# Moving the keys' products and sums of a seven-level complex scan from VectorE to GpSimd

## What is computed

```python
c = jax.lax.complex(qkva[..., 0], qkva[..., 1])
q, k, v, a = (c[..., 0], c[..., 1], c[..., 2], c[..., 3])
mag2 = a.real * a.real + a.imag * a.imag
a = a * (jax.lax.rsqrt(mag2) * jax.nn.sigmoid(jnp.log(mag2)))
kv = jnp.einsum('blhd,blhe->blhde', k, v)
...
def comb(c1, c2):
    a1, x1 = c1
    a2, x2 = c2
    return (a1 * a2, a2 * x1 + x2)
_, h = jax.lax.associative_scan(comb, (a_e, kv), axis=1)
y = jnp.einsum('blhd,blhde->blhe', q, h)
```

## Time and profile before

| | |
|---|---|
| time, median of 3 runs | 3893.76 us (3890.83 to 3897.11) |
| profiled execution, its own time | 3925.24 us |
| span of the profiled execution | 3923.4 us |
| TensorE busy | 2883.7 us (73%) |
| VectorE busy | 2113.1 us (54%), 4928 instructions |
| ScalarE busy | 928.3 us (24%) |
| GpSimd busy | 652.6 us (17%), 682 instructions |
| mean granted TensorE clock | 0.78 of full speed |
| L2075 (scores), per head group | 205.6 and 203.4 us busy, 232.2 and 226.2 us idle before |

### The profile page before, as it was taken

One profiled execution on the slowest core, in us unless ns is written; L12 is line 12 of the kernel. 1 busy time (PEld: TensorE's weight loads), 2 busy tenths in 40 slices (PEclk: granted clock), 3 DMA queues, 4 the chain that ended last, 5 costly groups with the idle time before them and its releaser, 6 DMA issues.

```text
span 3923.4 us, 112483 instructions
## 1 busy us (share of the span) xinstructions
PE 2883.7 (73%) x51136; PEld 2151.2 (55%) x51136; DVE 2113.1 (54%) x4928; ACT 928.3 (24%) x1820; POOL 652.6 (17%) x682
## 2 busy tenths in 40 slices
PE   4268669867885898488749875986678466999990
PEld 3254357435743674466447545743564346888880
DVE  4446766576658556856685577658543841000004
ACT  0212133113311431142223213311321131222220
POOL 0314200410060006002500330042000000000006
PEclk8578767867786878587858776886769578999995
DMA  2122201210021122012201220121011005555545
GB/s 78 22 55 49 45 3 50 65 30 33 30 66 20 40 39 59 10 39 50 49 9 40 60 45 4 44 65 32 9 46 41 4 15 189 198 195 191 197 156 174
DMA packets 230141, 249.52 MB, mean 64 GB/s; under 512 B 147360, under 2 KB 187168, under 8 KB 227360
## 3 DMA queue, kind: packets, MB, share of 16 engines
q1 hardware_dynamic: 223520, 225.54, 20.1%
q0 software_dynamic: 6144, 16.79, 1.4%
HBM read 196.15 MB, written 46.14 MB: 62 GB/s over the span
## 4 chain that ended last, share of the span: by engine, by line
PE 63%; issue 14%; DVE 8%; POOL 5%; ACT 4%; DMA 1%; SPq 0%; POOLq 0%; DVEq 0%
PE bank L1780 13%; PE bank L2075 10%; PE bank L2278 7%; PE bank L2297 7%; PE bank L2013 4%; POOL arena L1672 3%; PE bank L2090 2%; PE bank L2095 2%; PE bank L1790 2%; PE bank L1907 2%; POOL arena L1716 2%; PE bank L1912 2%; PE bank L1917 1%; PE bank L2035 1%; PE bank L1886 1%
## 5 line engine op out<-in xcount | busy, mean ns | idle before, releaser
L1672 POOL TENSOR_TENSOR arena<-arena 128x1 f32<-128x1 f32 (+30 forms) x496 | 435.1, 907 | 639.4 <-DMA arena<-n_d 467.9
L2075 PE MATMUL bank<-arena 32*32 32x32 f32 (+1 forms) x13824 | 205.6, 253 | 232.2 <-issue 226.0
L2075 PE MATMUL bank<-arena,xn 32*32 32x32 f32 (+1 forms) x13824 | 203.4, 258 | 226.2 <-issue 226.2
L1693 POOL DMA_INDIRECT h_d<-h_tok,pos_now x64 | 66.2, 1035 | 1753.5 <-DVE pos_now L1537 1736.5
L1128 DVE TENSOR_REDUCE arena<-arena 128x1 f32<-128x1 f32 (+30 forms) x496 | 243.7, 502 | 173.3 <-POOL arena L1672 168.9
L1780 PE MATMUL bank<-hT,ring 128*128 128x512 f32 x640 | 316.1, 647 | 8.2 <-DVE arena L1272 8.2
L2075 PEld LDWEIGHTS bank<-arena 32*32 32x32 f32 x13824 | 181.8, 134 | 254.3 <-issue 241.2
L2075 PEld LDWEIGHTS bank<-arena,xn 32*32 32x32 f32 x13824 | 179.3, 135 | 242.6 <-issue 242.1
L2278 PE MATMUL bank<-arena 128*128 128x256 f32 x1248 | 276.6, 380 | 0.0
L2297 PE MATMUL bank<-arena 128*128 128x256 f32 x1248 | 275.6, 379 | 0.0
L2278 PEld LDWEIGHTS bank<-arena 128*128 128x128 f32 x1248 | 237.7, 191 | 32.8 <-issue 0.4
(11 more groups left out here) (332 smaller groups left out, 5185.8 us busy)
## 6 DMA issues: line engine op xcount, KB each, us to landing
arena<-in_w_ring SPq DMA_DIRECT2D x78, 1024.0 KB, 5.0
ring<-in_w_ring SPq DMA_DIRECT2D x104, 512.0 KB, 4.9
arena<-h_d SPq DMA_DIRECT2D x39, 256.0 KB, 5.3
y_d<-arena SPq DMA_DIRECT2D x39, 256.0 KB, 5.8
n_d<-NA SPq DMA_DIRECT2D x8, 1024.0 KB, 3.9
arena<-n_d SPq DMA_DIRECT2D x16, 512.0 KB, 8.1
u_d<-arena SPq DMA_DIRECT2D x8, 1024.0 KB, 3.8
NA<-u_d SPq DMA_DIRECT2D x32, 256.0 KB, 5.9
```

What stands on the lines that cost most here:

```text
L1672: pool.tensor_tensor(part, Usub[:, c, 0:t, 0:t], Nsub[:, c, t, 0:t].unsqueeze(1).to_broadcast([P, t, t]), ALU.mult)\
L2075: i_ = mm(bank[4 * hg + h][keys, b * width:(b + 1) * width], K2[rows_, r, b, keys], q, start=(r == 0), stop=(r == 1), skip_group_check=True)
```

## The change

The two key products and the two key sums of each step are issued on GpSimd instead of VectorE, in a loop behind the clearing of the score buffers. They write the same buffers u1 and u2. GpSimd waits for the table (`a_ok`), for the key planes in level 0, for its own previous results, and for `scored` before the sums; it now raises `k_ready`. SyncE and ScalarE, which waited for `k_ready` alone, wait for VectorE's `q_ready` too, since both engines have to be through. Queries, tables, masked copies and all matmuls are as before.

```diff
@@ sync
                 if pre and rest:
                     sp.wait_ge(*at(k_ready, 1))
+                    sp.wait_ge(*at(q_ready, 2 * HG + 1))
                     load_next()
@@ scalar
                     act.wait_ge(*at(k_ready, HG * LEVELS))
+                    act.wait_ge(*at(q_ready, HG * (STEPS + 1)))
@@ vector
-                        Ta = w[:, :, :, 1]
-                        kk = K2s[hg][:, :, :, :].rearrange(half, two=2, m=m)[:, :, :, 0]
-                        if lev == 0:
-                            dve.wait_ge(*at(plane_ok, 6 * hg + 6))
-                        dve.tensor_tensor(tmp(u1), kk, over(Ta[:, 0]), ALU.mult).then_inc(*up(dve_step, me))
-                        dve.tensor_tensor(tmp(u2), kk, over(Ta[:, 1]), ALU.mult).then_inc(*up(dve_step, me))
                         settle()
                         dve.wait_ge(*at(scored, 2 * (lev + 1) + hg + 1))
                         step(dve.tensor_tensor(q_hi, tmp(t1), tmp(t2), ALU.add))
                         dve.tensor_scalar(q_lo[:, 0], q_hi[:, 1], -1.0, None, ALU.mult).then_inc(*up(q_ready, me))
-                        dve.tensor_tensor(kk[:, 0], tmp(u1)[:, 0], tmp(u2)[:, 1], ALU.subtract)
-                        dve.tensor_tensor(kk[:, 1], tmp(u1)[:, 1], tmp(u2)[:, 0], ALU.add).then_inc(*up(k_ready, me))
@@ gpsimd
+                    def turn_key_columns(hg, lev):
+
+                        m = 1 << lev
+                        w = level_table(hg, lev).rearrange("p r (j two) -> p r j two", two=2)
+                        later = w[:, :, :, 1]
+                        kk = K2s[hg][:, :, :, :].rearrange("p r b (n two m) -> p r (b n) two m", two=2, m=m)[:, :, :, 0]
+
+                        def over(v):
+                            return v.unsqueeze(1).unsqueeze(3).to_broadcast([P, 2, NT // (2 * m), m])
+
+                        v1, v2 = [u[:, :, 0:NT // 2].rearrange("p r (n m) -> p r n m", m=m) for u in (u1, u2)]
+                        if lev == 0:
+                            pool.wait_ge(*at(plane_ok, 6 * hg + 6))
+                            pool.wait_ge(*at(a_ok, hg + 1))
+                        else:
+                            pool.wait_ge(*at(a_ok, 2 * lev + hg + 1))
+                        settle()
+                        pool.tensor_tensor(v1, kk, over(later[:, 0]), ALU.mult).then_inc(*up(key_part, me))
+                        pool.tensor_tensor(v2, kk, over(later[:, 1]), ALU.mult).then_inc(*up(key_part, me))
+                        settle()
+                        pool.wait_ge(*at(scored, 2 * (lev + 1) + hg + 1))
+                        pool.tensor_tensor(kk[:, 0], v1[:, 0], v2[:, 1], ALU.subtract)
+                        pool.tensor_tensor(kk[:, 1], v1[:, 1], v2[:, 0], ALU.add).then_inc(*up(k_ready, me))
+
+                    for lev, hg in itertools.product(range(LEVELS), range(HG)):
+                        turn_key_columns(hg, lev)
```

More of the change, by code:

```diff
@@ L329, in build @@
         u_in = signal("u_in", nxt=64)
-        dve_step = signal("dve_step", rest=226, nxt=13, pre=36)
+        dve_step = signal("dve_step", rest=198, nxt=13, pre=36)
         pre_var = signal("pre_var", pre=1)
@@ L434, in build @@
         k_ready = signal("k_ready", rest=14)
+        key_part = signal("key_part", rest=28)
         numbered = signal("numbered")
@@ L1552, in turn @@
                              q_ready, masked, state_ok, hsq_ok, rt_var, rt_gap, hot_ok,
-                             pos_ok, k_ready])
+                             pos_ok])
                 dve.sem_inc(started.handle, 1)
@@ L1700, in turn @@
                     settle()
-                counted(seg, [zeroed, sub_mul])
+                counted(seg, [zeroed, sub_mul, key_part, k_ready])
                 pool.sem_inc(started.handle, 1)
```

## The result

The changed kernel takes **3939.57 us** (median of 4 runs, 3922.45 to 3942.26) against 3892.30 for the kernel before on the same chip (3890.12 to 3897.11). The ratio is 1.0108, with an interval of [1.0081, 1.0134]: slower by some 42 to 47 us, where 55 were forecast. Run again on another chip, the ratio was 1.0105 [1.0089, 1.0122].

What follows compares the result with a forecast made beforehand. TensorE's own issue paces levels 0 to 4, and the scan's tail decides the change. 48 us of tail plus 7 of clock make 55, against the median 3893.76 giving 3949 us (+1.4%); range 3902 to 4000.

Steps and rivals of the forecast that it cites:

- The bound of the scan's body: Levels 0 to 4: TensorE's own issue sets the pace, 7.5 us a step; lag stays under 4.8 us of margin.
- Freed time on VectorE: 28 us per segment leave VectorE, but only two key sums before the last copies count: 0.67 us, 5.4 in eight.
- GpSimd's own cost: Key work on GpSimd: 1.27 us per 512-element product, 0.73 per 256-element sum, 4.0 us a step.
- Exclusion and alternation: VectorE's two-SBUF-input instructions and GpSimd's reads take turns, so a late step needs 2.59 plus 4.0, together 6.6 us.
- The rival without exclusion: Both engines run side by side in the scan, leaving only the 0.67 us gain: 3888.4 us; chance 0.09.
- the one in which VectorE wins each contest: Rival: in the scan's tail GpSimd is held off and step 11's key sum is late: 11 us, 3905; chance 0.17.
- The tail, 6.0 us a segment: Scan's end: taking turns puts VectorE's step 12 query signal 22.7 us after step 9's query sum; 48 us in all.
- Who ends it: Last copies to first outputs take 20 us instead of 14.3, ended by VectorE's query signal and not by ScalarE.
- The clock, 0.9 us a segment: After a longer pause the outputs' first microseconds may run at TensorE's low clock: 0 to 1.7 us, 7 in all.
- The covers: SyncE's load, ScalarE's waits and GpSimd's row scatter move at no cost; uncovered, each would cost 1 to 3 us per segment.
- The sum: Whole kernel: 48 us plus 7 make 55 us, giving 3949 us (+1.4%).
- The dear GpSimd: Rival: GpSimd at 1.2 times the rows or winning each contest, levels 0 to 2 overflow: 3975 to 4000; chance 0.19.

Runs made afterwards that it cites:

- early: Changed kernel with the key work of levels 5 and 6 back on VectorE, levels 0 to 4 on GpSimd; ratio to the kernel before 0.9986.
- late: Changed kernel with only the key work of levels 5 and 6 on GpSimd, the first ten steps back on VectorE; ratio to the kernel before 1.0097.
- nokeys: Changed kernel with all key products and key sums left out, GpSimd only raising the signals; ratio to the kernel before 0.9987.
- copies_first: Kernel before, all work on VectorE, with each step's masked copies ahead of its two key sums; ratio to the kernel before 0.9986.
- hold: Kernel before, with TensorE waiting before the output products for VectorE's last query signal (step 13) instead of step 12's; ratio 1.0101.
- again: The unchanged kernel before, run once more as if it were a change, for a second profiled execution; ratio 1.0002.

## Why the prediction was right, point by point

**The bound of the scan's body**: right. 699.8 against 699.9 us, within some 5 us, and early and late show the margin holding.

**Freed time on VectorE**: right. 0.67 us a segment, 5.4 in all; nokeys and copies_first measured 5.1 and 5.5 (0.13% and 0.14% of 3912, each with 4 to 5 us of uncertainty).

**GpSimd's own cost**: too dear in the tail. I took 1.27 us for 512 elements from the solve's rows. The key products took 1.05 when nothing was in the way (1293.02), and behind a VectorE instruction only 0.92 from its end; a sum of 256 elements 0.73 as taken, and 0.58 from the other's end. I had allowed for such a credit at the handover on VectorE only.

**Exclusion and alternation**: right, and now shown: products at 1281 and 1352 ns, and 692 beside memsets. Of the three means for which I had named 1.0 to 1.6 us the query sum's falls short, at 0.84: 85 of the 112 kept their 0.69 us, among them every one that had waited for TensorE's scores. The rival without exclusion falls with it, and the one in which VectorE wins each contest falls by the order of time, one instruction each.

**The tail, 6.0 us a segment**: the mechanism was right and the size wrong; it is 4.0 us, 32 in eight (168.2 less 136.0). The parts: I let 15 GpSimd instructions in at 14.7 us, and 18 came in, the whole of step 13's too. With 0.92 and 0.58 for a blocked product and sum these 18 are 8 x 0.92 + 10 x 0.58 = 13.2 us. On VectorE, 8.7 and 0.9 for the copies, less 0.14 at some 14 handovers, make 7.6: roughly 20.8, against the measured 20.9 from query sum to signal. So my 22.7 to the signal was off by errors that pulled against each other: a lower price of each turn (my 15 at the measured sizes are 7 x 0.92 + 8 x 0.58 = 11.1, so -3.6), three turns more (+2.1), the copies of step 9, which I had left out of VectorE's 8.7 (+0.9), four more handovers that give time back (-0.6), and my 0.7 for GpSimd's waits, for which the measured sum has no room (-0.7). That the sum came within 2 us is in part luck. The term that was mis-sized most is one GpSimd turn.

**Who ends it**: right. From the last copies (1293.09) to the outputs 18.8 us instead of 14.3 (forecast 20), ended by VectorE's signal.

**The clock, 0.9 us a segment**: right in kind, too small. Behind a pause of 3.8 us (after) or 4.0 (hold) the output matmuls begin at 0.68 us a group, go to 1.22 and are back at 0.71; the first four L2112 groups take 5.9 or more instead of 4.4 in all eight segments. From the start of its first output matmul to the end of its last, a segment takes 28.9 us in the mean against 27.7 (before) and 27.4 (again): 1.2 to 1.6 a segment, some 11 in all, in the upper half of my 0 to 1.7. The first four groups alone lose more, 1.5 to 2.8 us, and part of that is made up before the last. I had put the slow stretch at the very start of the outputs; it begins 1.2 to 1.3 us in.

**The covers**: right as a whole. hold has no key work on GpSimd and costs the same, so the waits of SyncE and ScalarE and the scatter behind the new part cost nothing measurable; the scatter still idles up to 126.3 us. Which of them has how much cover was not tried one by one.

**The sum**: 32 + 11 = 43 us against 41 to 47 measured (by the ratios and by the medians), where I had 48 + 7 = 55. The dear GpSimd and its 3975 us fall: levels 0 to 2 did not overflow.

## What to carry to other kernels

Before moving work to an engine that stands idle, ask what it reads beside whom: here, two-input VectorE instructions (and its TENSOR_SCALAR) and GpSimd instructions that read SBUF take turns, one each, so the move frees nothing while both have work, and it costs the sum of both where VectorE is on the chain. Such a move is free under another engine's bound and dear in the last microseconds before a stage change; a single wait that keeps the helper off until the critical signal is given took the whole loss back. And look first at what the freed time is worth: here 5 us, which the order of two statements gave as well.

## What I had not expected of the hardware

- The turns go by instructions, whatever their length, and each turn lasts as long as the other's instruction: a VectorE piece of 16 elements (0.16 us) waited 0.5 us for its turn, and a fifth GpSimd instruction a step added 0.5 us to the tail, not 4.
- A blocked instruction ends sooner after its release than it takes alone: 0.55 for 0.69 us on VectorE, 0.92 for 1.05 and 0.58 for 0.73 on GpSimd.
- 448 memsets of 0.74 to 0.95 us left VectorE's two-input products at 692 ns, but took turns with its TENSOR_SCALAR: 100 of them were stretched from 0.74 to 0.89 us by it, and ten of the TENSOR_SCALARs from 0.29 to 0.39 and more.
- TensorE's granted clock fell not in its pause but behind it: 1.00 in the first 1.3 us of the outputs, 0.57 in the next 4 us, though TensorE was busy without a gap. In hold it is the same without any key work on GpSimd. With pauses of up to 0.7 us before the outputs (all kernels with a tail of 17.4 us or less) the first four groups took 4.4 us in all eight segments; with 2.3 us and more, never under 5.8. No pause between these two was measured.
